# First attention layer: who scales the gathered rows, and who fetches one column of every fourth group

## The reference

```python
h = x @ W
e = leaky_relu(a_src[src] + a_dst[dst], 0.2)
m = segment_max(e, dst)
ex = exp(e - m[dst])
alpha = ex / segment_sum(ex, dst)[dst]
out = segment_sum(alpha[:, None] * h[src], dst) + bias
```

## Time and profile before

| | |
|---|---|
| median of 3 runs | 7078.87 us (7066.26 to 7079.29) |
| the profiled execution's own time | 7064.06 us |
| its span | 7062.3 us |
| sweep a, first to last gather of POOL | 316.1 to 2273.9 us |
| sweep b, first to last gather | 2648.0 to 4548.8 us |
| sweep rel, first to last gather | 5002.4 to 6902.7 us |
| busy: POOL, DVE, ACT, PE | 4988.8, 3415.4, 987.5, 608.1 us |

### The profile page before, as it was taken

One profiled execution on the slowest core, in us unless ns is written; L12 is line 12 of the kernel. 1 busy time (PEld: TensorE's weight loads), 2 busy tenths in 40 slices (PEclk: granted clock), 3 DMA queues, 4 the chain that ended last, 5 costly groups with the idle time before them and its releaser, 6 DMA issues. The chain is left out here.

```text
span 7062.3 us, 57439 instructions
## 1 busy us (share of the span) xinstructions
PE 608.1 (9%) x2404; PEld 419.6 (6%) x2404; DVE 3415.4 (48%) x6209; ACT 987.5 (14%) x3084; POOL 4988.8 (71%) x5250
## 2 busy tenths in 40 slices
PE   1100000000000540000000000068311000000000
PEld 1100000000000430000000000034200000000000
DVE  8465666656566566444444444478222222222223
ACT  2222222222222130000000000057100000000000
POOL 5777777777776657777777777632577777777776
PEclk7555555555555665555555555579655555555555
DMA  5367676776766524444444444355333333333333
GB/s 186 107 213 221 210 224 209 221 218 216 224 206 202 171 84 126 118 119 118 118 119 119 124 119 118 101 181 206 136 109 108 109 111 110 110 108 109 108 108 96
DMA packets 344911, 1045.33 MB, mean 148 GB/s; under 512 B 111529, under 2 KB 139564, under 8 KB 306594
## 3 DMA queue, kind: packets, MB, share of 16 engines
q1 hardware_dynamic: 157746, 670.54, 26.6%
q0 software_dynamic: 172192, 365.19, 20.5%
q10 hardware_dynamic: 14544, 5.93, 0.3%
HBM read 527.27 MB, written 513.96 MB: 147 GB/s over the span
## 5 line engine op out<-in xcount | busy, mean ns | idle before, releaser
L1151 POOL DMA_INDIRECT edge_rows<-table_a,src_i x1568 | 1481.2, 945 | 477.8 <-issue 477.8
L2096 POOL DMA_INDIRECT edge_rows<-table_rel,rel_row x1523 | 1436.8, 943 | 506.7 <-issue 462.6
L1151 POOL DMA_INDIRECT edge_rows<-table_b,src_i x1523 | 1437.2, 944 | 464.8 <-issue 464.8
L2178 DVE TENSOR_TENSOR edge_rows<-edge_rows,ps 128x1024 f32<-128x1024 f32 x195 | 238.1, 1221 | 1386.2 <-DMA edge_rows<-table_rel,rel_row 1382.8
L1293 DVE TENSOR_TENSOR z<-edge_rows,dst_logit 128x16 f32<-128x16 f32 (+1 forms) x196 | 40.7, 208 | 1591.5 <-DMA edge_rows<-table_b,src_i 942.9
L1274 DVE TENSOR_TENSOR edge_rows<-edge_rows,ps 128x1032 f32<-128x1032 f32 (+1 forms) x390 | 484.1, 1241 | 86.6 <-ACT edge_rows L1208 69.5
L1269 DVE TENSOR_TENSOR ps<-edge_rows,ps 128x1032 f32<-128x1032 f32 (+1 forms) x390 | 485.7, 1245 | 8.6 <-ACT edge_rows L1208 1.9
L1208 ACT ACTIVATE edge_rows<-edge_rows,weight_decay 128x129 f32<-128x129 f32 x1568 | 470.2, 389 | 0.0
L878 PE MATMUL ps<-ident,edge_rows 128*128 128x128 f32 x16 | 3.9, 426 | 3480.6 <-DVE edge_rows L1274 2032.0
L1211 ACT ACTIVATE ps<-weight_decay 128x128 f32<-128x128 f32 x98 | 27.5, 281 | 1809.3 <-DVE weight_decay L1313 1809.3
L2127 ACT ACTIVATE ps<-keep 128x16 f32<-128x16 f32 x98 | 19.6, 201 | 1852.1 <-DVE edge_rows L2178 1846.6
(11 more groups left out here) (294 smaller groups left out, 3164.6 us busy)
## 6 DMA issues: line engine op xcount, KB each, us to landing
sums_a<-edge_rows SPq DMA_DIRECT2D x98, 2064.0 KB, 8.2
sums_b<-edge_rows SPq DMA_DIRECT2D x98, 1120.0 KB, 4.6
edge_rows<-in_ea SPq DMA_DIRECT2D x98, 1024.0 KB, 11.8
sums_rel<-edge_rows SPq DMA_DIRECT2D x98, 1024.0 KB, 4.2
table_rel<-rel SPq DMA_DIRECT2D x98, 512.0 KB, 3.0
edge_rows<-table_b SPq DMA_DIRECT2D x2880, 0.5 KB
edge_rows<-table_b ACTq DMA_DIRECT2D x2880, 0.5 KB
edge_rows<-table_rel ACTq DMA_DIRECT2D x2880, 0.5 KB
```

Source lines behind the costliest of these rows:

```text
L1151: e.indirect_dma_start(out=rows[:, s, i, 0:L.W], out_offset=None, in_=L.table, in_offset=bass.IndirectOffsetOnAxis(ap=src[:, at:at + 1], a ...
L2096: e.indirect_dma_start(out=rows[:, s, i, :], out_offset=None, in_=table_rel, in_offset=bass.IndirectOffsetOnAxis(ap=rel_row[:, at:at + 1], ...
L2178: i = e.tensor_tensor(steps(g)[:, t, :, :], steps(g)[:, t, :, :], old, ALU.add)
```

## The change

- In sweep a ACT no longer scales the rows. It takes both exponentials with one instruction into PSUM, and DVE multiplies all 16 columns with one instruction, as in sweep b.
- In sweep a the last column of every fourth group (`every(4, 7)`: groups 7, 11, ..., 95, 23 of them) is no longer gathered by POOL; ACT alone fetches its 128 rows, one quarter in each of four groups: after the exponential of group g it fetches rows 0 to 31 of group g + 4, or 32 to 63 of g + 3, or 64 to 95 of g + 2, or 96 to 127 of g + 1, whichever of these groups is helped.
- `keep` is copied one group earlier, to two places in PSUM.
- In all sweeps the 32 indices of a fetch are loaded to registers behind the fetch before it (`prepare`), no longer right ahead of their use.
- One more row of indices is turned at the start (`helped_src` has two sets).

```diff
-        def fetch(self, e, regs, g, p0, n):
+        def prepare(self, e, regs, g, p):
+
+            if g in self.place:
+                h = self.place[g]
+                e.load(regs, self.index[h:h + 1, p:p + len(regs)])
+
+        def fetch(self, e, regs, g, p):
 
             if g not in self.place:
                 return
             h, s = self.place[g], g % self.NS
             e.wait_ge(*self.stored[s].at(16 * (g // self.NS)))
             e.wait_ge(*self.summed.at(g - self.NS + 2))
-            for p in range(p0, p0 + n, len(regs)):
-                m = min(len(regs), p0 + n - p)
-                e.load(regs[0:m], self.index[h:h + 1, p:p + m])
-                for i in range(m):
-                    row = e.snap(regs[i])
-                    e.dma_start(self.rows[p + i:p + i + 1, s, LAST, 0:self.W], self.table[bass.ds(row, 1), :]
-                                ).then_inc(self.fetched[h % 3].sem, 16)
+            for i, reg in enumerate(regs):
+                row = e.snap(reg)
+                e.dma_start(self.rows[p + i:p + i + 1, s, LAST, 0:self.W], self.table[bass.ds(row, 1), :]
+                            ).then_inc(self.fetched[h % 3].sem, 16)
...
-        helped = Helped(L.name, helped_b if L.AE else {}, helped_src, L.table, L.W, rows, NS, stored, summed)
+        helped = Helped(L.name, helped_b if L.AE else helped_a, helped_src[:, 1 if L.AE else 0, :], L.table, L.W, rows, NS,
+                        stored, summed)
...
                 if L.AE:
-                    helped.fetch(e, regs_sync, g + 4, 0, P // 4)
-                    helped.fetch(e, regs_sync, g + 3, P // 4, P // 4)
+                    helped.fetch(e, regs_sync, g + 4, 0)
+                    helped.fetch(e, regs_sync, g + 3, P // 4)
+                    helped.prepare(e, regs_sync, g + 5, 0)
+                    helped.prepare(e, regs_sync, g + 4, P // 4)
...
+                e.wait_ge(*for_exp.at(g + 1))
+                e.activation(factors, at, ACT.Exp).then_inc(exped.sem, 1)
                 if attr is not None:
-                    if g >= 1:
-                        e.wait_ge(*attr_summed.at(g))
-                    e.activation(keep_now, group_columns(keep[:, :], g), ACT.Copy).then_inc(keep_copied.sem, 1)
-                e.wait_ge(*for_exp.at(g + 1))
-                if H == 1:
-                    e.activation(at[:, 0, :, :], at[:, 0, :, :], ACT.Exp).then_inc(weight_exped.sem, 1)
-                    e.activation(factors[:, 1, :, :], at[:, 1, :, :], ACT.Exp).then_inc(exped.sem, 1)
-                    e.wait_ge(*weight_exped.at(g + 1))
-                    for i in range(GC):
-                        done = e.activation(R[:, i, 0:NW], R[:, i, 0:NW], ACT.Copy, scale=wd[:, g % 2, 0, i, :])
-                    done.then_inc(weighted.sem, 1)
-                else:
-                    e.activation(factors, at, ACT.Exp).then_inc(exped.sem, 1)
+                    if g + 1 < NG:
+                        copy_keep(g + 1)
+                    for i in range(4):
+                        helped.fetch(e, regs_scalar, g + 4 - i, i * P // 4)
+                    for i in range(4):
+                        helped.prepare(e, regs_scalar, g + 5 - i, i * P // 4)
...
-                if H > 1:
-                    t_weight = then(e.tensor_tensor(heads(R), heads(R), bc(factors[:, 0, :, :].unsqueeze(3), [P, GC, H, C + 1]),
-                                                    ALU.mult))
-                    join_step.append(t_weight)
+                t_weight = then(e.tensor_tensor(heads(R), heads(R), bc(factors[:, 0, :, :].unsqueeze(3), [P, GC, H, C + 1]),
+                                                ALU.mult))
+                join_step.append(t_weight)
```

More of the change, by code:

```diff
@@ L163, in build @@
     cut = sb_edges("cut", [P, EC])
-    helped_src = sb_edges("helped_src", [P, P], I32)
+    helped_src = sb_edges("helped_src", [P, 2, P], I32)
     spread = sb_edges("head_spread", [B.H + 1, B.WN])
@@ L215, in helped_columns @@
         return ap[:, at[0]:at[-1] + 1:at[1] - at[0]]
-    helped_b = every(2, 7)
+    helped_a, helped_b = every(4, 7), every(2, 7)
     class Helped:
@@ L225, in __init__ @@
             self.by_pool = {g: 16 * sum(GC - (i in place) for i in range(g % NS, g + 1, NS)) for g in range(NG)}
-            self.fetched = [sem(f"{name}_helped{i}") for i in range(3)] if place else []
+            self.fetched = [sem(f"{name}_helped{i}") for i in range(3)]
         def all_by_pool(self, slot):
             return self.by_pool[max(g for g in range(NG) if g % self.NS == slot)]
-        def fetch(self, e, regs, g, p0, n):
+        def prepare(self, e, regs, g, p):
[3 more added lines that the diff above has]
+        def fetch(self, e, regs, g, p):
             if g not in self.place:
@@ L464, in graph_stage @@
         hc = sb("head_count", [P, GK])
-        helped_f = sb("helped_f", [P, 2, P])
+        helped_f = sb("helped_f", [P, 3, P])
         helped_floated, helped_turned = sem("helped_floated"), sem("helped_turned")
@@ L636, in edge_places @@
                 e.wait_ge(*step.at(step.n))
-                e.tensor_copy(helped_f[:, 0, 0:len(helped_b)], helped_columns(tmp_e, helped_b)).then_inc(helped_floated.sem, 1)
+                for i, place in enumerate((helped_a, helped_b)):
+                    e.tensor_copy(helped_f[:, i, 0:len(place)], helped_columns(tmp_e, place)).then_inc(helped_floated.sem, 1)
                 e.wait_ge(*zero_stored.at(N_ZERO))
@@ L727, in vector @@
             e.wait_ge(*helped_turned.at(1))
-            then(e.tensor_copy(helped_src[:, :], ps[:, 7, 0:P]))
-            then(e.tensor_copy(helped_rel[:, :], ps[:, 7, P:2 * P]))
+            then(e.tensor_copy(helped_src[:, :, :].rearrange("p i c -> p (i c)"), ps[:, 7, 0:2 * P]))
+            then(e.tensor_copy(helped_rel[:, :], ps[:, 7, 2 * P:3 * P]))
         def tensor(e):
@@ L736, in tensor @@
                     table.t_turn(e, i)
-            e.wait_ge(*helped_floated.at(2))
-            for i in range(2):
+            e.wait_ge(*helped_floated.at(3))
+            for i in range(3):
                 done = e.transpose(ps[:, 7, i * P:(i + 1) * P], helped_f[:, i, :], ident[:, :])
@@ L1121, in attention_edges @@
             old_attr = ps[:, 5:7, :].rearrange("p b (t d) -> p (b t) d", d=D)
-            keep_now = ps[:, 3, 0:GC].rearrange("p (t k) -> p t k", t=GS)
+            keep_now = ps[:, 3:5, 0:GC].rearrange("p i (t k) -> p i t k", t=GS)
             keep_copied = sem_of("keep_copied", NG)
@@ L1194, in scalar, with copy_keep @@
         def scalar(e):
+            def copy_keep(g):
+                if g >= 2:
+                    e.wait_ge(*attr_summed.at(g - 1))
+                e.activation(keep_now[:, g % 2, :, :], group_columns(keep[:, :], g), ACT.Copy).then_inc(keep_copied.sem, 1)
+            if attr is not None:
+                copy_keep(0)
             for g in range(NG):
@@ L1214, in scalar @@
                                  group_columns_of_heads(edge_logit[:, :, :], g), ACT.Copy).then_inc(terms_copied.sem, 1)
-                    helped.fetch(e, regs_scalar, g + 3, P // 2, P // 4)
-                    helped.fetch(e, regs_scalar, g + 2, 3 * P // 4, P // 4)
+                    helped.fetch(e, regs_scalar, g + 3, P // 2)
+                    helped.fetch(e, regs_scalar, g + 2, 3 * P // 4)
+                    helped.prepare(e, regs_scalar, g + 4, P // 2)
+                    helped.prepare(e, regs_scalar, g + 3, 3 * P // 4)
             crossing.scalar(e)
@@ L1265, in join @@
                     e.wait_ge(*step.at(join_step[-1]))
-                if H == 1 and g == 0:
-                    e.wait_ge(*weighted.at(1))
                 decay_now = factors[:, 1, t * GK:(t + 1) * GK, :]
@@ L2128, in scalar @@
                              ).then_inc(keep_copied.sem, 1)
-                helped.fetch(e, regs_scalar, g + 2, P // 2, P // 4)
-                helped.fetch(e, regs_scalar, g + 1, 3 * P // 4, P // 4)
+                helped.fetch(e, regs_scalar, g + 2, P // 2)
+                helped.fetch(e, regs_scalar, g + 1, 3 * P // 4)
+                helped.prepare(e, regs_scalar, g + 3, P // 2)
+                helped.prepare(e, regs_scalar, g + 2, 3 * P // 4)
         def tensor(e):
```

11 lines of the change are left out of this document (3 added, 8 removed).

## The result

The changed kernel took 7378.7 us (median of 4 runs, 7369.5 to 7379.1), the kernel before in the same comparison 7078.7 us: ratio 1.0422, interval 1.041 to 1.0435. The profiled execution took 7369.5 us, 305.4 more than before's 7064.1. Forecast were 7274 us and slower, with a range of 7038 to 7460: the way and the mechanism were right, and the size was 210 of 305 us.

What follows compares the result with a forecast made beforehand. POOL's gathers bound sweep a; ACT's fetches would replace them: 15.0 + 60.4 + 10.35 + 1.35 + 2.5 = 89.6 us a round against 79.9, 23 rounds +223, end -13, so +210 us: 7274 us, range 7038 to 7460.

Steps and rivals of the forecast that it cites:

- POOL's pace was the bound, and four fetches in a row on ACT took its place: Sweep a: ACT's round of 89.6 us replaces POOL's 79.9 us for four groups; chance 0.72.
- The multiplication: Sweep a, DVE: one added instruction of 2064 elements per group, 2.30 us, hidden mid-sweep, showing once at the end.
- The round: Sweep a, from one helped group's start to the next, four groups later: 89.6 us, against 79.9 before.
- four fetches: ACT in sweep a: four fetches of 32 rows per round, 15.1 us each, 60.4 us together.
- three loads, exponentials and copies: ACT's queue in a round: three register loads 10.35 us (2.15 and two of 4.1), exponentials and copies 1.35 us.
- landing: End of a round: the last fetched row lands 2.5 us later, taken from SP's small loads.
- I take +2.0: ACT's fetch in sweep a: 2.0 us added to 13.1 for the burst of store and attribute load, giving 15.1.
- the faster rival: Sweep a: ACT's round fits into POOL's 78.7 us and the kernel gets faster, 7038 us; chance 0.15.
- The moved loads: Sweeps b and rel: loading registers behind the fetches changes the order, not the sum, and costs nothing.
- ACT keeps up: Rival, sweep a: four fetches and three loads take at most 59.9 us, kernel at 7038 us; chance 0.15.
- The burst holding ACT as it held SP: Rival, sweep a: each fetch takes 19.9 us, the round 108.8, the kernel 7716 us; chance 0.07.
- DVE as the bound: Rival, sweep a: the added multiplication makes DVE the bound, needing a group over 18.7 us against 15.0; no own chance.

Runs made afterwards that it cites:

- e1: The changed kernel without helped groups in sweep a (POOL gathers all columns, DVE multiplies, moved loads stay), against the kernel before: ratio 1.0005.

## Why the prediction was right

**POOL's pace was the bound, and four fetches in a row on ACT took its place:** right. Removing the fetches gives 1.0005; moving half of them gives 0.9961.

**The multiplication:** 2.30 us forecast, 2.30 measured, hidden.

**The round, by its terms** (forecast, then measured in the round shown):

| term | forecast | measured |
|---|---|---|
| start of the helped group to the first fetch | 15.0 | 14.9 (1617.16 to 1632.10) |
| four fetches | 60.4 | 64.0 (15.76 + 15.57 + 16.24 + 16.47) |
| three loads, exponentials and copies | 10.35 + 1.35 = 11.7 | 8.1 (2.86 + 2.61 + 2.60) |
| landing | 2.5 | 6.05 |
| sum | 89.6 | 93.1 |

The landing in the table is that of the round before the one shown (1611.11 to 1617.16). Three terms were mis-sized. The fetch: "I take +2.0", it is +3. The loads: I gave two of them 4.1 us because a burst would be beside them; they start some 8 us behind the store, the slow rows end 6 us behind it, and the median is 2.3. The landing: I took 2.5 from SP's small loads; the rows land 6.05 us behind the fetch, and after 3.0 with small attributes. The errors of the fetches (+3.6) and of the loads (-3.6) cancel, which is luck; the landing's (+3.5) is what is left. The range, 422 us wide, took in the faster rival's time too, so that the time fell into it says little; the round, 89.6 us forecast and 93.0 measured, says more.

**From the round to the time.** From group 3 to group 95 there are 23 rounds of +13.1 us, +301 (forecast +223). Group 3 itself, ahead of all fetches, starts 8.6 us later (407.5 against 398.9): POOL's first gather starts 2.2 us later (318.33 against 316.11), and of the early and late arrivals that alternate group 3 now has a late one (26.1 us behind group 2, before 14.7). It has a late one with the multiplication alone too (404.6); what decides it stays open. Behind group 95 the sweep takes 44.6 us, forecast 45.2, before 58.1: -13.5. The last join ends at 2591.24, 296.6 us later than before. The forecast for it was 210: 23 rounds 3.4 us too short make 78 of the missing 87, group 3's start the rest. The other 9 us of the span are not in sweep a: 1 is between sweeps b and rel, and 4 each are in sweeps b and rel, whose gathers are 947 ns long in this execution and 944 before and in all experiments but one (946). Why an execution has the one or the other stays open; the code of those gathers did not change.

**The moved loads** of sweeps b and rel: at nothing, as forecast (e1: 1.0005).

**The rivals.** ACT keeps up: not as written, but it does where SP has the first of the four fetches (0.9963). The burst holding ACT as it held SP (6.8 us more in each fetch): no; a row behind a store takes about 1 us and four or five do, which makes 3. The longest single row took 1.27 us. The Trainium skill ("Perfetto Trace Analysis", DMA Instruction — HWDGE) has the descriptor generator locked while it is used, with the wait for the lock in the profiled time of a DMA; the trace shows rows of 1 us in place of 0.23 and no single long hold, and it shows no lock for itself. DVE as the bound: no (1.0005 with the multiplication alone).

**Open.** What exactly holds the four or five rows behind a store was not isolated: no run changes the store's size, and behind stores that closely follow an attribute load the rows are not held.

## What to carry to other kernels

When work is handed to an engine with idle time, follow its queue in program order through one whole period: 32 small DMAs are 13 to 16 us during which that engine answers nobody, and its short instruction behind them may be what another engine waits for. Add the chain up from one release to the next, landing included, and compare it with the period of the bound; under it the chain is free, over it every microsecond counts in every round. Splitting the same DMAs over two queues turned +4.2% into -0.4%; leaving four groups without them in between turned it into -0.2%.

## What the runs showed of the hardware

- The issuing of 32 DMAs of one 520-byte row by ACT took 12.6 us undisturbed (0.39 us each), 16.0 in the changed kernel, where SP issued a 2 MB store within them or right ahead of them: about four rows of 1 us each, with 1 MB or 128 KB loaded behind the store alike. Where SP had issued an attribute load less than 8 us before the store, 32 DMAs took 13 us with a store within them too.
- A load of 32 registers took 2.1 to 2.5 us where it came 7 us and more behind a store, and 5.1 to 7.3 us on ACT right behind a 2 MB store. The Trainium skill ("Runtime: NRT & Kernel Launch", Instruction fetch mechanics) has about 200 ns for each register, by which 32 would be an estimated 6.4 us: no load that far from a store took as long.
- A DMA of 104 KB behind one of 1 MB in the same queue was issued in 2.15 us in the rows above (SP fetching three quarters), 7.16 at the sweep's start and up to 9.93 with two queues, against 0.34 some 8 us later.
